# Reordering VectorE's instructions in the first batch of a fused attention and mixture-of-experts kernel

## The chip, the cores and the metric

The kernel runs on one core of one Trainium2 chip. The metric is the device time of one execution in microseconds, the median of several runs. The core's engines work side by side and wait for each other by semaphores: TensorE (matmul), VectorE, ScalarE, GpSimd, and SyncE, which here only starts transfers.

## The reference

The input x has 4 images of 128 channels and 32 × 32 points. Three blocks follow each other, all in float32:

```
h = group_norm(x)                      # 32 groups, eps 1e-6, scale and bias per channel
q, k, v = nin(h, Wq, bq), nin(h, Wk, bk), nin(h, Wv, bv)
w = softmax(q^T k * C**-0.5)           # 1024 x 1024 per image
x = x + nin(w v, Wp, bp)
t = tokens(x)                          # (4, 1024, 128)
t = t + linear_attention(layer_norm(t))      # 4 heads of 32, softmax of the keys over the tokens
t = t + top2_of_8_experts(layer_norm(t))     # gelu(t w1 + b1) w2 + b2, weighted by the router
```

## The kernel before

The work is ordered by hand. Each engine has its own program, written out in the order in which the engine is to work, and each of them has an `opening_batch` for image 0, a `batch` for images 1 to 3, and a last part with the experts. Semaphores link the engines; an engine that reaches a wait stops there with all that stands behind it.

Products of full precision are made of three matmuls with operands split in a high and a low part. ScalarE makes the high part out of PSUM (q_hi, k_hi, v_hi, pT_hi), then VectorE subtracts it to get the low part (q_lo, k_lo in `project`, L1037; v_lo in `project_v`, L1028; pT_lo in `turn_probs`, L1059). k_hi and k_lo are the two halves of one tile, k_both, so rows name them k_both. Halves of 512 points are named by a digit: q0, q1, k0, k1.

Attention of one image has 8 row tiles of 128 rows. For row tile i TensorE makes the scores (`score`, six matmuls, L1449 to L1451), VectorE takes scale and row maximum (`row_maximum`, L1052, 128 × 1024), ScalarE the exponential (`softmax`, L720), TensorE transposes the probabilities (T{i}, L1464), ScalarE and VectorE split them (L726, L1059). After tiles 0 to 3's transposes the attention products begin (`attend`). The first score needs the low parts of q0 and k0, its second half that of k1. The score of tile 2 needs the maximum of tile 0.

The group statistics of images 1 to 3 are taken in image 0 on VectorE: `group_stats(b)` is two BN_STATS (L935) on x of image b, held in the tiles gel, hs and out_s. They go into one `channel_means(1, 3)` (L941) after the third, then over TensorE (group_means) and back to VectorE (group_deviation, group_variance, group_affine), and from there to GpSimd, which normalizes image 1. `setup_rest` (L1019 to L1022) takes the router's rows and b1 out of the PSUM bank in which TensorE turned them (rowsT); the second half of the transposed x (xT1) goes into the same bank and waits for that. TensorE's order there is: scores 0 and 1, v, T0, score 2, rowsT, T1, x transposed (xT0, xT1), score 3, T2, score 4, the group means, T3, the group variances, score 5, attend.

Of the kernel before, what the change touches and what calls it, by code (L numbers as in the profile page):

```python
# [132 lines left out]
def conv_attention_moe(nc, x, gn_scale, gn_bias, wq, bq, wk, bk, wv, bv, wp, bp,  # L133
# [28 lines left out]
    with ctx:  # L162
# [170 lines left out]
        def ps(place, unit):  # L333
            bank = place.bank(unit)
            return ring[:, bank, :] if bank < 4 else scores[:, bank - 2, :]

        def wait_filled(eng, place, unit):
            eng.wait_ge(filled[place.bank(unit)], place.earlier(unit) + 1)
# [13 lines left out]
        def half(m, n):  # L352
            return m[:, n * BANK:(n + 1) * BANK]
# [559 lines left out]
        def _(dve):  # L913
# [3 lines left out]
            def after(ins):  # L917
                made[0] += 1
                ins.then_inc(dve_chain, 1)
                dve.wait_ge(dve_chain, made[0])  # L920
# [11 lines left out]
            def group_stats(b):  # L932
                for n in range(HALVES):
                    dve.wait_ge(ld_x0b if (b, n) == (0, 1) else ld_x[b], 16)
                    last = dve.bn_stats(gst[:, b, n, :], half(x_of[b], n))  # L935
                after(last)

            def channel_means(b0, nb):

                for b in range(b0, b0 + nb):  # L940
                    last = dve.bn_aggr(gmv[:, b, :], gst[:, b, :, :])  # L941
                last.then_inc(gn_mv, 1)

            def group_deviation(place, b0, nb):

                mean, dev = gsum[:, 0, b0:b0 + nb], gsum[:, 1, b0:b0 + nb]
                wait_filled(dve, place, "gn_mean")
                dve.tensor_copy(mean, ps(place, "gn_mean")[:, 0:nb]).then_inc(drained[place.bank("gn_mean")], 1)
                wait_drained(dve, place, "gn_mean")
                after(dve.tensor_tensor(dev, gmv[:, b0:b0 + nb, 0], mean, ALU.subtract))  # L950
                after(dve.tensor_tensor(dev, dev, dev, ALU.mult))
                dve.tensor_tensor(dev, dev, gmv[:, b0:b0 + nb, 1], ALU.add).then_inc(gn_mv, 1)

            def group_variance(place, b0, nb):
                wait_filled(dve, place, "gn_var")
                dve.tensor_copy(gsum[:, 2, b0:b0 + nb], ps(place, "gn_var")[:, 0:nb]
                                ).then_inc(drained[place.bank("gn_var")], 1)

            def group_affine(n, b0, nb):

                dve.wait_ge(gn_rstd, n)
                after(dve.tensor_scalar(gmul[:, b0:b0 + nb], gsum[:, 3, b0:b0 + nb], gs_c, None, ALU.mult))
                after(dve.tensor_tensor(gadd[:, b0:b0 + nb], gsum[:, 0, b0:b0 + nb], gmul[:, b0:b0 + nb], ALU.mult))
                dve.tensor_scalar(gadd[:, b0:b0 + nb], gadd[:, b0:b0 + nb], -1.0, gb_c, ALU.mult, ALU.add
                                  ).then_inc(gn_made, 1)
# [35 lines left out]
            def weights_again():  # L1001

                split(wq_raw, wq_hi[:, :], wq_lo[:, :])
                split(wk_raw, wk_hi[:, :], wk_lo[:, :])
# [11 lines left out]
            def setup_rest():  # L1016

                wait_filled(dve, FIRST, "rowsT")
                dve.tensor_copy(b1_c[:, :], ps(FIRST, "rowsT")[:, E:2 * E])  # L1019
                dve.tensor_copy(router_top[:, 0:E], ps(FIRST, "rowsT")[:, 0:E])  # L1020
                after(dve.tensor_copy(router_two[:, 0:E], ps(FIRST, "rowsT")[:, 0:E]))
                dve.tensor_tensor(router_two[:, E:2 * E], ps(FIRST, "rowsT")[:, 0:E],  # L1022
                                  router_two[:, 0:E].bitcast(FP32), ALU.subtract).then_inc(drained[FIRST.bank("rowsT")], 1)

            def low(place, unit, hi, lo, made, count):

                dve.wait_ge(made, count)
                dve.tensor_tensor(lo, ps(place, unit)[:, 0:lo.shape[-1]], hi.bitcast(FP32), ALU.subtract  # L1028
                                  ).then_inc(drained[place.bank(unit)], 1)

            def project(place, b, unit, hi, lo, bias):
                n = int(unit[1])
                if place is FIRST:
                    bias = bias_first[:, 0:1] if unit[0] == "q" else bias_first[:, 1:2]

                dve.wait_ge(qk_hi_made, b * 4 + ATTENTION["qk"].index(unit) + 1)
                dve.scalar_tensor_tensor(out=half(lo, n), in0=ps(place, unit), scalar=bias,  # L1037
                                         in1=half(hi, n).bitcast(FP32), op0=ALU.add, op1=ALU.subtract
                                         ).then_inc(drained[place.bank(unit)], 1)

            def project_v(place, b):
                for n in range(HALVES):
                    low(place, f"v{n}", half(v_hi, n), half(v_lo, n), v_hi_made, b * HALVES + n + 1)

            def row_maximum(place, b, i):

                if i >= 2:
                    wait_filled(dve, place, f"T{i - 2}b")
                elif place is not FIRST:
                    wait_filled(dve, place, f"T{TILES - 2 + i}b")  # L1050
                dve.wait_ge(s_made, b * TILES + i + 1)
                dve.tensor_scalar(prob[:, i % 2, :],  # L1052
                                  scores[:, 2 * (i % 2):2 * (i % 2) + 2, :].rearrange("p a t -> p (a t)"),
                                  -SCALE, None, ALU.mult, ALU.min, accum_out=row_max[:, i:i + 1]).then_inc(s_max, 1)

            def turn_probs(place, b, i):
                for n, unit in enumerate((f"T{i}a", f"T{i}b")):
                    dve.wait_ge(p_hi_made, b * (2 * TILES) + 2 * i + n + 1)
                    dve.tensor_tensor(tile_group(pT_lo, n, i), as_tiles(ps(place, unit)),  # L1059
                                      tile_group(pT_hi, n, i).bitcast(FP32), ALU.subtract  # L1060
                                      ).then_inc(drained[place.bank(unit)], 1)

            def invert_sums(b, g):

                dve.wait_ge(s_exp, b * TILES + (g + 1) * QUAD)
                dve.reciprocal(row_sum[:, 1, g * QUAD:(g + 1) * QUAD], row_sum[:, 0, g * QUAD:(g + 1) * QUAD]
                               ).then_inc(r_made, 1)
# [150 lines left out]

            def opening_batch(place, b):
                project(place, b, "q0", q_hi, q_lo, bq_c)  # L1220
                group_stats(1)
                project(place, b, "k0", k_hi, k_lo, bk_c)
                project(place, b, "k1", k_hi, k_lo, bk_c)
                group_stats(2)
                project(place, b, "q1", q_hi, q_lo, bq_c)
                row_maximum(place, b, 0)
                row_maximum(place, b, 1)
                project_v(place, b)
                turn_probs(place, b, 0)
                row_maximum(place, b, 2)  # L1230
                setup_rest()
                turn_probs(place, b, 1)
                group_stats(3)
                channel_means(1, B - 1)
                row_maximum(place, b, 3)
                turn_probs(place, b, 2)
                group_deviation(place, 1, B - 1)
                turn_probs(place, b, 3)
                group_variance(place, 1, B - 1)
                row_maximum(place, b, 4)  # L1240
                invert_sums(b, 0)
                group_affine(2, 1, B - 1)
                weights_again()
                row_maximum(place, b, 5)
                turn_probs(place, b, 4)
                row_maximum(place, b, 6)
                turn_probs(place, b, 5)
                row_maximum(place, b, 7)
                dve.wait_ge(experts_split, 3)
                residual(place, b, 0)  # L1250

            def batch(place, b, la, lc):
# [57 lines left out]
                take_g(place)  # L1310

            opening_batch(FIRST, 0)
            batch(SECOND, 1, 0, None)
            with dve.Fori(2, B) as b:
# [572 lines left out]
```

## Time and profile before

| | |
|---|---|
| median of 3 runs | 318.69 us (318.09 to 318.78) |
| span of the profiled execution, first to last instruction | 315.6 us |
| TensorE matmul busy | 297.7 us, 94% |
| VectorE busy | 254.9 us, 81% |
| ScalarE busy | 200.8 us, 64% |
| GpSimd busy | 154.1 us, 49% |
| granted TensorE clock, mean | 1.000 |

A profile describes one execution; for this one the page gives its span and no device time of its own. Times in rows count from the span's start. "Busy" is time in which an instruction was in work. Instructions of one engine overlap a little at their ends, so the time an instruction takes of its engine is the distance from its start to the next start, when nothing waits.

### The profile page before, as it was taken

The numbers are of one execution on the slowest core, as the hardware profiler recorded it, in microseconds if no ns is written. First come the engines' busy times: TensorE is split into PE (matmuls) and PEld (weight loads), VectorE is DVE, ScalarE is ACT, GpSimd is POOL, SyncE is SP. The second block draws the span as 40 slices with busy tenths as digits, with TensorE's granted clock in tenths as the row PEclk, the third lists the DMA queues.
The fourth block names the chain that finished last, engine by engine and source line by source line (L and its number), as shares of the span: only waits on it lengthen the run. The fifth ranks groups of instructions, "written<-read, shape, count | busy, mean of one in ns | idle before, by whom it ended". The sixth has DMA issues, their size and how long they took to land.

```text
span 315.6 us, 5504 instructions
## 1 busy us (share of the span) xinstructions
PE 297.7 (94%) x1584; PEld 238.3 (76%) x1584; DVE 254.9 (81%) x635; ACT 200.8 (64%) x352; POOL 154.1 (49%) x358
## 2 busy tenths in 40 slices
PE   5898989989999999999999999998799998999996
PEld 4776768866878887878887797875677786668885
DVE  4599686587587799987698887999598896999996
ACT  3447474566771587663279577468578645888882
POOL 2899593059941985980784300599604049200000
PEclk9999999999999999999999999999999999999999
DMA  5902000010000021000000118395321783229801
GB/s 136 330 12 70 0 1 2 0 66 2 1 3 0 0 69 39 30 12 0 0 1 0 66 38 271 117 391 212 124 86 67 279 300 119 75 87 375 295 7 66
DMA packets 12904, 29.61 MB, mean 94 GB/s; under 512 B 2208, under 2 KB 6224, under 8 KB 10960
## 3 DMA queue, kind: packets, MB, share of 16 engines
q1 hardware_dynamic: 12448, 28.87, 26.3%
q10 hardware_dynamic: 432, 0.46, 0.4%
q8 instruction: 10, 0.16, 0.2%
q14 instruction: 14, 0.11, 0.1%
HBM read 24.73 MB, written 4.59 MB: 93 GB/s over the span
## 4 chain that ended last, share of the span: by engine, by line
PE 66%; DVE 13%; POOL 9%; ACT 7%; issue 3%; DMA 1%; DVEq 0%; POOLq 0%
PE ring L1464 11%; PE ring L1449 7%; PE ring L1451 7%; PE ring L1450 7%; PE scores L1449 6%; PE scores L1451 6%; PE scores L1450 6%; POOL w_n L589 3%; PE ring L1805 3%; POOL u L589 3%; ACT pT_hi L726 3%; ACT prob L720 2%; PE ring L1604 2%; DVE pT_lo L1059 2%; PE ring L1591 2%
## 5 line engine op out<-in xcount | busy, mean ns | idle before, releaser
L867 ACT ACTIVATE gel<-scores,b_c 128x512 f32<-128x512 f32 x64 | 43.9, 689 | 19.5 <-PE scores L1451 18.0
L1059 DVE TENSOR_TENSOR pT_lo<-ring,pT_hi 128x512 fp32r<-128x512 f32 x64 | 40.5, 681 | 9.8 <-ACT pT_hi L726 9.4
L720 ACT ACTIVATE prob<-prob,row_max 128x1024 f32<-128x1024 f32 x32 | 36.8, 1149 | 14.2 <-DVE prob L1052 14.2
L580 POOL TENSOR_SCALAR rstd<-lmv 128x4 f32<-128x4 f32 x16 | 4.3, 266 | 82.3 <-DVE lmv L1094 81.1
L1052 DVE TENSOR_SCALAR_CACHE_REDUCE prob<-scores 128x1024 f32<-128x1024 f32 x32 | 38.6, 1214 | 3.3 <-PE scores L1451 3.3
L726 ACT ACTIVATE pT_hi<-ring 128x512 fp32r<-128x512 f32 x64 | 34.6, 599 | 10.3 <-PE ring L1464 9.9
L1464 PE MATMUL ring<-ident,prob 128*128 128x128 f32 x256 | 33.7, 275 | 3.6 <-ACT prob L720 1.9
L1464 PEld LDWEIGHTS ring<-ident,prob 128*128 128x128 f32 x256 | 28.7, 140 | 8.5 <-ACT prob L720 3.7
L1449 PE MATMUL scores<-wT_hi,w_hi 128*128 128x512 f32 x64 | 29.3, 458 | 0.0
L1449 PE MATMUL scores<-k_both,q_hi 128*128 128x512 f32 x64 | 26.9, 421 | 1.9 <-DVE k_both L1037 1.3
L1449 PE MATMUL ring<-pT_hi,v_hi 128*128 128x512 f32 x64 | 26.5, 415 | 0.8 <-DVE pT_lo L1059 0.8
L1451 PE MATMUL scores<-k_both,q_lo 128*128 128x512 f32 x64 | 25.2, 393 | 0.0
L1451 PE MATMUL scores<-wT_hi,w_lo 128*128 128x512 f32 x64 | 25.1, 392 | 0.0
L1450 PE MATMUL scores<-wT_lo,w_hi 128*128 128x512 f32 x64 | 25.1, 392 | 0.0
L1450 PE MATMUL scores<-k_both,q_hi 128*128 128x512 f32 x64 | 25.1, 392 | 0.0
L1451 PE MATMUL ring<-pT_hi,v_lo 128*128 128x512 f32 x64 | 25.0, 391 | 0.0
L1450 PE MATMUL ring<-pT_lo,v_hi 128*128 128x512 f32 x64 | 25.0, 390 | 0.0
L611 POOL TENSOR_TENSOR t<-t,bout_row 128x128 f32<-128x128 f32 x32 | 14.0, 476 | 18.4 <-PE scores L1464 10.8
L730 ACT ACTIVATE o_s<-ring 128x512 f32<-128x512 f32 x8 | 4.8, 598 | 24.7 <-PE ring L1451 24.7
L589 POOL TENSOR_SCALAR u<-t,rstd 128x128 f32<-128x128 f32 x32 | 18.8, 608 | 0.9 <-POOL rstd L584 0.9
L589 POOL TENSOR_SCALAR w_n<-t,rstd 128x128 f32<-128x128 f32 x32 | 17.2, 555 | 0.9 <-POOL rstd L584 0.9
L584 POOL TENSOR_TENSOR rstd<-rstd,minus_half 128x4 f32<-128x4 f32 x16 | 16.6, 1040 | 0.0
(300 smaller groups left out, 780.9 us busy)
## 6 DMA issues: line engine op xcount, KB each, us to landing
pT_hi<-scratch_s SPq DMA_DIRECT2D x8, 1024.0 KB, 7.6
prob<-scratch_s SPq DMA_DIRECT2D x4, 1024.0 KB, 7.2
k_both<-scratch_s SPq DMA_DIRECT2D x3, 1024.0 KB, 5.8
z_in<-scratch_z SPq DMA_DIRECT2D x8, 256.0 KB, 2.9
out_dram<-out_s SPq DMA_DIRECT2D x7, 256.0 KB, 2.2
xb<-in_x_dram SPq DMA_DIRECT2D x3, 512.0 KB, 3.3
scratch_z<-out_s SPq DMA_DIRECT2D x2, 512.0 KB, 2.8
k_both<-scratch_s SPq DMA_DIRECT2D x4, 256.0 KB, 4.2
```

The lines of the kernel that those rows point to most:

```text
L584: pool.tensor_tensor(std[:, tiles], std[:, tiles], minus_half[:, tiles], ALU.pow).then_inc(ln_small[n], 1)
L589: last = pool.tensor_scalar(dst[:, j, :], src[:, j, :], neg[:, j:j + 1], std[:, j:j + 1], ALU.add, ALU.mult)
L611: last = pool.tensor_tensor(tiles_piece(t2, n), tiles_piece(t1, n), tiles_piece(bout_b, n), ALU.add)
L720: act.activation(prob[:, i % 2, :], prob[:, i % 2, :], ACT.Exp, bias=row_max[:, i:i + 1], scale=-1.0, accum_out=row_sum[:, 0, i:i + 1]).th ...
L726: act.activation(tile_group(pT_hi, n, i), as_tiles(ps(place, unit)), ACT.Copy).then_inc(p_hi_made, 1)
L867: act.activation(half(gel, s % 2), scores[:, s % 2, :], ACT.Gelu, bias=b1_c[:, s % E:s % E + 1]).then_inc(e_gelu, 1)
L1052: dve.tensor_scalar(prob[:, i % 2, :], scores[:, 2 * (i % 2):2 * (i % 2) + 2, :].rearrange("p a t -> p (a t)"), -SCALE, None, ALU.mult, AL ...
L1059: dve.tensor_tensor(tile_group(pT_lo, n, i), as_tiles(ps(place, unit)), tile_group(pT_hi, n, i).bitcast(FP32), ALU.subtract).then_inc(drai ...
L1449: pe.matmul(dst, lh, rh, start=start, stop=False)
L1450: pe.matmul(dst, lh, rl, start=False, stop=False)
L1451: return pe.matmul(dst, ll, rh, start=False, stop=stop)
L1464: last = pe.transpose(dst[0:t.shape[-1], j * step:j * step + rows], t, ident[0:rows, 0:rows])
```

## The change

VectorE's program for image 0 is written in another order. The low parts of k0 and k1 come directly after that of q0, the maximum of row tile 0 ahead of q1's low part, and the statistics of images 1 and 2 after the maximum of tile 1 and after that of tile 2. All other engines keep their order, and no instruction's work changes.

```diff
             def opening_batch(place, b):
                 project(place, b, "q0", q_hi, q_lo, bq_c)
-                group_stats(1)
                 project(place, b, "k0", k_hi, k_lo, bk_c)
                 project(place, b, "k1", k_hi, k_lo, bk_c)
-                group_stats(2)
+                row_maximum(place, b, 0)
                 project(place, b, "q1", q_hi, q_lo, bq_c)
-                row_maximum(place, b, 0)
                 row_maximum(place, b, 1)
+                group_stats(1)
                 project_v(place, b)
                 turn_probs(place, b, 0)
                 row_maximum(place, b, 2)
+                group_stats(2)
                 setup_rest()
                 turn_probs(place, b, 1)
                 group_stats(3)
```

VectorE's order before, from q0's low part to the maximum of row tile 3 (gel and hs hold x of images 1 and 2):

```order
L1037 SCALAR_TENSOR_TENSOR q_lo<-ring,bias_first,q_hi 128x512
L935 BN_STATS gst<-gel 128x6 x2
L1037 SCALAR_TENSOR_TENSOR k_both<-ring,bias_first,k_both 128x512 x2
L935 BN_STATS gst<-hs 128x6 x2
L1037 SCALAR_TENSOR_TENSOR q_lo<-ring,bias_first,q_hi 128x512
L1052 TENSOR_SCALAR prob,row_max<-scores 128x1024 x2
L1028 TENSOR_TENSOR v_lo<-ring,v_hi 128x512 x2
L1059 TENSOR_TENSOR pT_lo<-ring,pT_hi 128x4x128 x2
L1052 TENSOR_SCALAR prob,row_max<-scores 128x1024
L1019 COPY b_c<-ring 128x8
```

The same place after the change, up to the same row:

```order
L1037 SCALAR_TENSOR_TENSOR q_lo<-ring,bias_first,q_hi 128x512
L1037 SCALAR_TENSOR_TENSOR k_both<-ring,bias_first,k_both 128x512 x2
L1052 TENSOR_SCALAR prob,row_max<-scores 128x1024
L1037 SCALAR_TENSOR_TENSOR q_lo<-ring,bias_first,q_hi 128x512
L1052 TENSOR_SCALAR prob,row_max<-scores 128x1024
L935 BN_STATS gst<-gel 128x6 x2
L1028 TENSOR_TENSOR v_lo<-ring,v_hi 128x512 x2
L1059 TENSOR_TENSOR pT_lo<-ring,pT_hi 128x4x128 x2
L1052 TENSOR_SCALAR prob,row_max<-scores 128x1024
L935 BN_STATS gst<-hs 128x6 x2
L1019 COPY b_c<-ring 128x8
```

Both pairs of statistics moved down past TensorE's first scores, and both still stand ahead of the router's rows (the COPY) and so ahead of the maximum of row tile 3, which follows further down in both. In between, these rows stand in both:

```order
L1022 TENSOR_TENSOR router_two<-ring,router_two 128x8
L1059 TENSOR_TENSOR pT_lo<-ring,pT_hi 128x4x128 x2
L935 BN_STATS gst<-out_s 128x6 x2
L941 BN_AGGR gmv<-gst 128x2 x3
L1052 TENSOR_SCALAR prob,row_max<-scores 128x1024
```

Nothing moved there.

## Rows read from the trace of the kernel before

**Rows 1.** The page: the span, and what each engine was busy.

```profile
span 315.6 us, 5504 instructions
PE 297.7 (94%) x1584; PEld 238.3 (76%) x1584; DVE 254.9 (81%) x635; ACT 200.8 (64%) x352; POOL 154.1 (49%) x358
```

**Rows 2.** The chain of waits from 12 to 32 us: start, us, what.

```profile
13.95 0.29 DVE gst L935
...
28.80 1.09 ACT pT_hi L726 x2
29.88 1.13 ACT prob L720 x2
```

**Rows 3.** VectorE in order of time, image 0: start, us, instruction, idle before it.

```profile
13.20 0.75 DVE L1037 SCALAR_TENSOR_TENSOR q_lo<-ring,bias_first,q_hi 128x512 fp32r<-128x512 f32 x1 [0.97 <-ACT q_hi L709]
13.86 1.28 DVE L935 BATCH_NORM_STATS2 gst<-gel 128x6 f32<-128x512 f32 x2
15.18 1.41 DVE L1037 SCALAR_TENSOR_TENSOR k_both<-ring,bias_first,k_both 128x512 fp32r<-128x512 f32 x2
16.50 1.28 DVE L935 BATCH_NORM_STATS2 gst<-hs 128x6 f32<-128x512 f32 x2
...
18.48 1.21 DVE L1052 TENSOR_SCALAR_CACHE_REDUCE prob<-scores 128x1024 f32<-128x1024 f32 x1
...
20.77 0.08 DVE L1052 DVE_READ_ACCUMULATOR prob<-scores 128x1 f32 x1
21.49 1.29 DVE L1028 TENSOR_TENSOR v_lo<-ring,v_hi 128x512 fp32r<-128x512 f32 x2 [0.65 <-ACT v_hi L715]
...
23.89 1.22 DVE L1052 TENSOR_SCALAR_CACHE_REDUCE prob<-scores 128x1024 f32<-128x1024 f32 x1
...
25.04 0.16 DVE L1019 COPY b_c<-ring 128x8 f32<-128x8 f32 x1
...
28.23 1.17 DVE L1052 TENSOR_SCALAR_CACHE_REDUCE prob<-scores 128x1024 f32<-128x1024 f32 x1
...
32.39 1.29 DVE L1059 TENSOR_TENSOR pT_lo<-ring,pT_hi 128x512 fp32r<-128x512 f32 x2 [0.89 <-ACT pT_hi L726]
```

**Rows 4.** ScalarE in order of time: k's high parts, exponentials of tiles 0, 3.

```profile
13.49 1.39 ACT L709 ACTIVATE k_both<-ring,bias_first 128x512 fp32r<-128x512 f32 x2 [0.33 <-PE ring L1451]
...
19.74 1.15 ACT L720 ACTIVATE prob<-prob,row_max 128x1024 f32<-128x1024 f32 x1 [4.17 <-DVE prob L1052]
...
29.77 1.15 ACT L720 ACTIVATE prob<-prob,row_max 128x1024 f32<-128x1024 f32 x1
```

**Rows 5.** TensorE's matmuls in order of time: projection, then score of tile 0.

```profile
12.49 0.63 PE L1450 MATMUL ring<-h_lo,wk_hi 128*128 128x512 f32 x1
...
12.92 0.47 PE L1451 MATMUL ring<-h_hi,wk_lo 128*128 128x512 f32 x1
...
16.07 0.47 PE L1449 MATMUL scores<-k_both,q_hi 128*128 128x512 f32 x1 [1.29 <-DVE k_both L1037]
...
17.31 0.40 PE L1451 MATMUL scores<-k_both,q_lo 128*128 128x512 f32 x1
```

**Rows 6.** Later, a score's last matmul and the maximum that waited for it.

```profile
86.45 0.39 PE L1451 MATMUL scores<-k_both,q_lo 128*128 128x512 f32 x1
86.98 1.23 DVE L1052 TENSOR_SCALAR_CACHE_REDUCE prob<-scores 128x1024 f32<-128x1024 f32 x1 [0.66 <-PE scores L1451]
```

**Rows 7.** TensorE's weight loads: xT1, score 3, T2, first attention product.

```profile
25.60 0.42 PEld L1464 LDWEIGHTS ring<-ident,xb 128*128 128x128 f32 x4 [0.20 <-DVE router_two L1022]
25.98 0.19 PEld L1449 LDWEIGHTS scores<-k_both,q_hi 128*128 128x128 f32 x1
...
28.10 0.85 PEld L1464 LDWEIGHTS ring<-ident,prob 128*128 128x128 f32 x8 [0.88 <-issue]
...
33.73 0.19 PEld L1449 LDWEIGHTS ring<-pT_hi,v_hi 128*128 128x128 f32 x1 [0.39 <-DVE pT_lo L1059]
```

**Rows 8.** GpSimd in order of time: it takes up image 1's columns.

```profile
35.91 0.29 POOL L540 COPY affine<-gmul 128x1 f32<-128x1 f32 x1 [0.93 <-DVE gadd L964]
```

## The prediction

> **What bounds the kernel now.** The page comes first: TensorE is at work for 94% of a span of 315.6 us [rows 1]. Yet a share over the whole span says nothing about the first 30 us, which is all that the change touches, so I went to the chain of waits for that stretch. It is an unbroken run of pieces: statistics on VectorE at 13.95, the keys' low parts, the first maxima, and by the end ScalarE's conversion of row tile 2 at 28.80 and its exponential of row tile 3 behind it, ending at 31.01 [rows 2]. The chain's last two pieces on ScalarE hide something that the third view, VectorE alone in order of time, shows. VectorE stands still once between 13.20 and 28.23: for 0.65 us, waiting for the high part of v [rows 3]. Counted from the start of one instruction to the start of the next, that wait is 21.49 − 20.77 = 0.72 us. No other row of VectorE in that stretch has idle time ahead of it. TensorE, in contrast, idles 1.29 us ahead of its first score [rows 5]. So VectorE sets the pace here, and the key quantity is how long VectorE stands still, not how early any one thing is made.
>
> How near is ScalarE behind it? The maximum of tile 3 starts at 28.23. In a place where ScalarE waits for nothing else, the exponential starts 19.74 − 18.48 = 1.26 us after its maximum [rows 3, 4], so the exponential of tile 3 could have begun at 29.49. It begins at 29.77, behind the conversion of tile 2. ScalarE covers 0.28 us of VectorE lateness, no more (0.33 if I count this maximum's own, shorter duration of 1.17 us against 1.21).
>
> **The change, part by part.** Nothing is added or removed. VectorE's instructions are the same, so its work from 13.20 to the maximum of tile 3 is the same 15.03 − 0.72 = 14.31 us. Both moved pairs of statistics (1.32 us a pair, 15.18 − 13.86 [rows 3]) still stand ahead of that maximum, because group_stats(3), channel_means and the maximum of tile 3 keep their places. Its new start therefore depends only on the new waits:
>
> 1. The low part of k0 follows the low part of q0 directly. VectorE is free at 13.86, but ScalarE makes k0's high part from 13.49 and k1's behind it, 1.39 us for both, so the first is there at 14.18 and the second at 14.88 [rows 4]. With 0.03 us for the hand-over, my estimate, k0 starts at 14.21 (wait 0.35 us) and k1 at 14.91, where 14.21 + 0.66 = 14.87 would be possible (wait 0.04 us; 0.66 is half of 16.50 − 15.18). Before, they ran from 15.18.
> 2. The first score waits for k0: before, the low part started at 15.18 and the score at 16.07, 0.89 us later [rows 3, 5]. Now 14.21 + 0.89 = 15.10. Its last matmul starts 17.31 − 16.07 = 1.24 us later, at 16.34. From a score's last matmul to its maximum there are 86.98 − 86.45 = 0.53 us in the one place of these rows where VectorE really waited for it [rows 6]. The maximum of tile 0 starts at about 16.86. VectorE was free at 14.91 + 0.66 = 15.57: wait 1.29 us. This is the stretch that the statistics used to fill.
> 3. Then q1's low part and the maximum of tile 1 follow at once, since score 1 starts its last matmul at 15.10 + 1.5 + 1.24 = 17.84 and allows its maximum at 18.37, while VectorE comes to it at 16.86 + 1.21 + 0.66 = 18.7. The first exponential starts at 16.86 + 1.26 = 18.12 instead of 19.74. The statistics of batch 1 then take VectorE to 21.2 (another 1.21 and 1.32), by when v's high part is long done (before, VectorE could take it 21.49 − 19.74 = 1.75 us after that exponential began, so now from 19.87): the old 0.72 us wait is gone.
> 4. Sum of waits after: 0.35 + 0.04 + 1.29 = 1.68 us, against 0.72. VectorE is 0.96 us behind the old order from there on. The maximum of tile 2 still gains, as one statistics pair now stands behind it: 23.89 + 0.96 − 1.32 = 23.53. Everything after that pair loses: the router's rows 25.04 → 26.00, the maximum of tile 3 28.23 → 29.19.
> 5. The exponential of tile 3 starts at 29.19 + 1.26 = 30.45, or 30.40 with the shorter duration, instead of 29.77: **0.63 to 0.68 us later**.
>
> TensorE's own path has to be checked too, since it waits for the router's rows before it turns the second half of x: weight load at 25.60, score 3 at 25.98, tile 2's transposes at 28.10 [rows 7]. Now 26.56, 26.94 and, with 1.5 us for a score, 28.44. The conversion of tile 2 then starts at about 29.14 and clears ScalarE at 30.1, 0.3 us ahead of the exponential. It doesn't set the time, but it is only 0.3 us away.
>
> From 30.4 on the old schedule repeats, shifted. The exponential releases tile 3's transposes, these the conversion, this VectorE's low part at 32.39 (VectorE idle 0.89 us there, so its 0.96 us of lateness is not added on top), and this the attention products, for which TensorE waits 0.39 us at 33.73 [rows 3, 7]. The same VectorE stretch then gives the affine columns for which GpSimd waits 0.93 us before it normalizes batch 1 [rows 8]. Both ways into the rest of the program shift alike, and the chain from there to the end is connected, with no clock-time event such as an early load to wait for. So I carry the 0.65 us undiminished: 315.6 + 0.65 = 316.25 us of span. The runs' median lies 3.09 us above the span; **318.69 + 0.65 = 319.34 us**. The page's row has no other time of its execution, so the span and this difference are the base.
>
> **The rivals.**
>
> *The head start is kept (not slower).* Place: VectorE's wait ahead of the maximum of tile 0. ScalarE's cover of 0.28 us makes a sum of waits of up to 0.72 + 0.28 = 1.00 us free; for that the wait on score 0 would have to be 0.6 us instead of 1.29. Then the time stays at 318.7 us. For it speaks that this wait is built from two hand-overs seen once each, and that the exponentials of tiles 0 and 1 do come over a microsecond earlier. Against it stand the 1.24 us of score 0 itself, which nothing shortens. A real gain needs something more, namely that the tile 3 exponential follows its forerunners; if the 1.0 us by which they lead survived, the time would be 317.7 us, but that asks VectorE to be done with the same work 1.0 us earlier than before, while it waits longer.
>
> *Part of the shift is absorbed.* The chain has pieces marked "issue" for which the profile shows no cause, and such pieces could shrink. Then 0 to 0.4 us remain: 318.7 to 319.1 us.
>
> *TensorE slows down.* In the new order TensorE, after tile 1's transposes and the first half of x, waits for the router's rows until 26.56. Before, that wait began at 25.60 − 0.20 = 25.40 [rows 7]; TensorE now comes to it 0.4 to 1.6 us sooner (the leads of the maximum of tile 2 and of the exponential of tile 0), say 1.2, so it idles 2.4 us instead of 0.20. Early in the trace, matmuls of this size start 12.92 − 12.49 = 0.43 us apart, the pitch of the 1.2 GHz level, against 1.24 / 5 = 0.25 in the first score [rows 5], the pitch of the 2.4 GHz level plus a late start. At the slow pitch, score 3 (six matmuls) costs 1.2 us more and the eight transposes some 0.4; less the 0.3 us of room, the shift grows by about 1.3 us: 320.6 us. Against it: idle of 1.29 us left the first score fast. The Trainium skill's page "TensorE: Matmul & The Clock Gate", Part 1 (The HAM clock gate), says that the array's rate is set by how busy it has been lately, and warns of idle gaps; by this rule the time could be the 320.6 us of this case. No row shown here has a gap of 2.4 us, so the trace of before neither bears the rule out nor speaks against it at this size.
>
> **How the numbers follow.** A difference of 0.2%, 0.64 us, is about what a measurement of this kernel can tell, and my sum ends just on it. The shift of 0.65 us undiminished has 0.74, of which slightly more than half reads as slower (0.39) and the rest as no change (0.35). Head start kept: 0.10, half of it a gain over 0.2%, half none. Absorbed in part: 0.09, no change. TensorE slows or something else makes it worse: 0.07, slower. That gives faster 0.05, same 0.49, slower 0.46. The range: unknowns of step 2 (the 0.53 us, by where VectorE catches the score) and of ScalarE's cover are ±0.15 us, the three runs of before spread over 0.7 us. To leave out no more than 2 in 10 it reaches to 318.5 below (absorbed, with the spread) and 320.0 above.
>
> **What would show it.** Right: k's low parts start near 14.2 and 14.9, the first score near 15.1, the maximum of tile 0 near 16.9 with a wait of about 1.3 us on the score ahead of it; no wait at v; TensorE idle over 2 us before the second half of x; the exponential of tile 3 near 30.4, now released by its maximum. Wrong: a maximum of tile 3 ahead of 28.9, or an unequal shift at 33.73 and at the end. A span under 315.6 would mean that the chain wasn't bound to VectorE where I say.

## The result, and the profile after

The changed kernel takes 320.88 us (median of 10 executions, 319.10 to 322.01) against 318.43 us for the kernel before beside it (10 executions, 317.08 to 319.89). The ratio is 1.0058, 95% interval 1.0033 to 1.0083: slower by 0.6%, where 0.2% was forecast. The two medians alone are 2.45 us apart (0.8%); the text goes by the ratio and its interval. The profiled execution has a span of 319.2 us against 315.6 us.

The first lines of the page, busy tenths in 40 slices of 8 us:

```profile
span 319.2 us, 5504 instructions
...
PE   5997998989999999999999999997899998999996
...
PEclk9997999999999999999999999999799999999999
```

TensorE's granted clock is no longer full everywhere: it falls in the fourth slice (24 to 32 us) and in the 29th (223 to 231 us). The row of before has 9 in all 40 slices. Over 24 to 32 us the mean granted clock is 0.79 here and 1.00 before. So the reader goes to TensorE in the fourth slice. Its matmuls in order of time, start, duration, idle ahead:

```profile
15.13 0.47 PE L1449 MATMUL scores<-k_both,q_hi 128*128 128x512 f32 x1 [0.34 <-DVE k_both L1037]
...
26.50 0.77 PE L1464 MATMUL ring<-ident,xb 128*128 128x128 f32 x4 [2.17 <-DVE router_two L1022]
26.91 0.78 PE L1449 MATMUL scores<-k_both,q_hi 128*128 128x512 f32 x1
27.49 0.63 PE L1450 MATMUL scores<-k_both,q_hi 128*128 128x512 f32 x1
27.92 0.63 PE L1451 MATMUL scores<-k_both,q_lo 128*128 128x512 f32 x1
...
29.62 1.38 PE L1464 MATMUL ring<-ident,prob 128*128 128x128 f32 x8
30.76 0.48 PE L1449 MATMUL scores<-k_both,q_hi 128*128 128x512 f32 x1
31.07 0.39 PE L1450 MATMUL scores<-k_both,q_hi 128*128 128x512 f32 x1
```

The first score starts 0.94 us earlier [rows 5], as meant. Then TensorE waits 2.17 us for the router's rows, and score 3 behind that wait runs with 0.43 us between starts (27.92 − 27.49), the pace of the 1.2 GHz level, until about 30.3; the mean granted clock from 26.5 to 30.3 us is 0.55. VectorE in order of time:

```profile
14.23 1.44 DVE L1037 SCALAR_TENSOR_TENSOR k_both<-ring,bias_first,k_both 128x512 fp32r<-128x512 f32 x2 [0.39 <-ACT k_both L709]
16.80 1.23 DVE L1052 TENSOR_SCALAR_CACHE_REDUCE prob<-scores 128x1024 f32<-128x1024 f32 x1 [1.13 <-PE scores L1451]
...
21.07 1.29 DVE L1028 TENSOR_TENSOR v_lo<-ring,v_hi 128x512 fp32r<-128x512 f32 x2
...
25.93 0.17 DVE L1019 COPY b_c<-ring 128x8 f32<-128x8 f32 x1
...
28.86 0.35 DVE L941 BATCH_NORM_AGGREGATE gmv<-gst 128x2 f32<-128x12 f32 x3
29.95 1.23 DVE L1052 TENSOR_SCALAR_CACHE_REDUCE prob<-scores 128x1024 f32<-128x1024 f32 x1 [0.74 <-PE scores L1451]
```

Up to the router's rows each start is within 0.1 us of the forecast (14.21, 16.86, no wait at v, 26.00). The maximum of tile 3 could have started at about 29.1 (forecast 29.19), but the slow score holds it until 29.95. On ScalarE:

```profile
18.07 1.15 ACT L720 ACTIVATE prob<-prob,row_max 128x1024 f32<-128x1024 f32 x1 [2.50 <-DVE prob L1052]
...
30.60 1.09 ACT L726 ACTIVATE pT_hi<-ring 128x512 fp32r<-128x512 f32 x2 [2.70 <-PE ring L1464]
31.57 1.15 ACT L720 ACTIVATE prob<-prob,row_max 128x1024 f32<-128x1024 f32 x1
```

Tile 0's exponential gains 1.67 us, tile 3's loses 31.57 − 29.77 = 1.80 us [rows 4]. From there the shift is carried rigidly for the next 57 us. The attention product on TensorE's weight loads, GpSimd's columns, and a maximum much later on VectorE:

```profile
35.53 0.19 PEld L1449 LDWEIGHTS ring<-pT_hi,v_hi 128*128 128x128 f32 x1 [0.39 <-DVE pT_lo L1059]
```

```profile
37.71 0.29 POOL L540 COPY affine<-gmul 128x1 f32<-128x1 f32 x1 [0.93 <-DVE gadd L964]
```

```profile
88.78 1.22 DVE L1052 TENSOR_SCALAR_CACHE_REDUCE prob<-scores 128x1024 f32<-128x1024 f32 x1 [0.66 <-PE scores L1451]
```

All three stand exactly 1.80 us later than in [rows 6, 7, 8], with the same idle time ahead of them. The span is 3.6 us longer, so the other 1.8 us have another origin: 0.2 us come in by 222 us (222.69 before, 224.68 after), without a cause found, and 1.6 us right behind that. Near 220 us TensorE waits 2.1 us for GpSimd, in both kernels. First before, then after:

```profile
222.69 0.66 PE L1464 MATMUL ring<-ident,u 128*128 128x128 f32 x4 [2.09 <-POOL u L589]
...
223.42 0.40 PE L1450 MATMUL scores<-wT_lo,w_hi 128*128 128x512 f32 x1
```

```profile
224.68 0.97 PE L1464 MATMUL ring<-ident,u 128*128 128x128 f32 x4 [2.08 <-POOL u L589]
...
225.88 0.63 PE L1450 MATMUL scores<-wT_lo,w_hi 128*128 128x512 f32 x1
```

The same wait, yet the slow pace follows only in the second. The change has no instruction near this wait. Is the fall chance of the execution? Only the mean granted clock is on record for every execution. The profiled executions with one such stretch have a mean of 0.994 or 0.995, the one with two has 0.989, so the others are counted by their means: 0.993 to 0.995 as one stretch, 0.988 or 0.989 as two. The mean doesn't say where the stretch lies.

| kernel | executions | clock 0.998 or more | one stretch | two |
|---|---|---|---|---|
| before (all comparisons below) | 84 | 26 | 53 | 5 |
| changed | 10 | 1 | 4 | 5 |

In the comparisons below, before has spans of 315.2 to 317.0 us at full clock and a median of 317.1 to 317.3 us over all. The profile of before that the prediction used was thus one of the fastest executions, not the typical one; its time would lie 1.7 to 2.2 us above its span, as in all profiled executions of the experiments, not 3.09.

### The profile page after: what moved, and what is told of

It reads as the page before. It is cut to its first block, busy times and chain, and to the rows that moved or that the text cites. A ratio compares the mean times of both kernels' runs of the same rounds, so it can differ in the third digit from the quotient of the medians.

```text
span 319.2 us, 5504 instructions
## 1 busy us (share of the span) xinstructions
PE 300.8 (94%) x1584; PEld 240.8 (75%) x1584; DVE 254.4 (80%) x635; ACT 200.6 (63%) x352; POOL 153.8 (48%) x358
## 4 chain that ended last, share of the span: by engine, by line
PE 65%; DVE 14%; POOL 9%; ACT 4%; issue 3%; DMA 3%; SPq 1%; DVEq 0%; POOLq 0%; ACTq 0%
PE ring L1464 11%; PE ring L1449 7%; PE ring L1451 7%; PE ring L1450 7%; PE scores L1449 7%; PE scores L1451 6%; PE scores L1450 6%; POOL w_n L589 3%; PE ring L1805 3%; POOL u L589 3%; DVE prob L1052 2%; ACT pT_hi L726 2%; DVE pT_lo L1059 2%; PE ring L1604 2%; PE ring L1591 2%
## 5 line engine op out<-in xcount | busy, mean ns | idle before, releaser
L1464 PEld LDWEIGHTS ring<-ident,prob 128*128 128x128 f32 x256 | 29.2, 142 | 7.5 <-ACT prob L720 3.3
L1449 PE MATMUL scores<-k_both,q_hi 128*128 128x512 f32 x64 | 27.5, 429 | 1.0 <-DVE prob L1052 0.7
L1450 PE MATMUL scores<-k_both,q_hi 128*128 128x512 f32 x64 | 25.6, 400 | 0.0
```

Of the source, the lines that this page charges most:

```text
L1449: pe.matmul(dst, lh, rh, start=start, stop=False)
L1450: pe.matmul(dst, lh, rl, start=False, stop=False)
L1464: last = pe.transpose(dst[0:t.shape[-1], j * step:j * step + rows], t, ident[0:rows, 0:rows])
```

## The experiments

The theory after the result: TensorE's longer idle ahead of xT1 costs it the clock in most executions (1.1 us), and VectorE's longer waits cost the rest (0.65 us). The rivals: the fall has another cause in the new order and would stay if the idle were filled; or the new order's place for the keys is what costs. A ratio below is always to before on the same chip, with its 95% interval.

**e1: TensorE kept busy in the early idle.**

```diff
-                turn_x(place, b)
+                pe.wait_ge(xb_made, b + 1)
+                turn(place, "xT0", [tile(xb, j) for j in range(QUAD)])
+                pe.wait_ge(s_max, 2)
+                for _ in range(16):
+                    pe.matmul(scores[:, 2, 0:C], group_mean[:, :], ident[:, :], start=True, stop=True)
+                turn(place, "xT1", [tile(xb, QUAD + j) for j in range(QUAD)])
```

> The changed kernel, with 16 small matmuls added on TensorE between the two halves of x's transposes, where it stood idle for 2.17 us; their output is overwritten. Theory (the idle costs the clock): all matmuls of score 3 start 0.23 us apart, granted clock 1.00 from 24 to 32 us, the maximum of tile 3 starts near 29.2 with no wait on the score, the exponential of tile 3 near 30.4 (changed kernel 31.57, before 29.77), and the time falls by about 1.1 us against the changed kernel, to 0.65 us above before. Rival (the slow stretch has another cause than this idle): the clock is still 0.79 there and the exponential stays near 31.5.

Measured: ratio 1.0064 (1.0042 to 1.0086), span of the profile 317.8 us. The filling missed its size: the 16 products became 32 matmuls. TensorE in the profile:

```profile
24.74 3.74 PE L1687 MATMUL scores<-ident,group_mean 128*128 128x128 f32 x32
28.32 0.60 PE L1464 MATMUL ring<-ident,xb 128*128 128x128 f32 x4
28.67 0.48 PE L1449 MATMUL scores<-k_both,q_hi 128*128 128x512 f32 x1
28.99 0.39 PE L1450 MATMUL scores<-k_both,q_hi 128*128 128x512 f32 x1
```

3.74 us of filling in place of 1.9 delayed xT1 to 28.32, so the time says nothing. The pace does: score 3 ran at full speed although it came 1.8 us later than in the changed kernel. It is repeated with half the filling as e7.

**e2: the router's rows ahead of image 2's statistics.**

```diff
                 row_maximum(place, b, 2)
+                setup_rest()
                 group_stats(2)
-                setup_rest()
```

> The changed kernel with the statistics of image 2 behind the router's rows instead of ahead of them, so that VectorE's work up to the maximum of tile 3 and its waits stay the same and only TensorE's wait for the rows shrinks from 2.17 to about 0.85 us. Theory: no fall of the clock; the exponential of tile 3 starts near 30.4, held by the maximum of tile 3 (29.2), so 0.65 us above before. Rival: the loss of the changed kernel comes from VectorE's order as such, so that the time stays near the changed kernel's, 1.8 us above before.

Measured: ratio 1.0024 (0.9998 to 1.0050); six of 12 executions at full clock with spans of 316.3 to 317.8 us. TensorE's wait and the third maximum on VectorE:

```profile
25.57 0.66 PE L1464 MATMUL ring<-ident,xb 128*128 128x128 f32 x4 [0.85 <-DVE router_two L1022]
...
26.30 0.40 PE L1450 MATMUL scores<-k_both,q_hi 128*128 128x512 f32 x1
```

```profile
29.53 1.17 DVE L1052 TENSOR_SCALAR_CACHE_REDUCE prob<-scores 128x1024 f32<-128x1024 f32 x1
```

With 0.85 us of idle the clock holds, and by the ratios the loss is less than half of the change's, though the two intervals overlap. The maximum stands 0.3 us later than expected (29.2); why, the section below says.

**e3: only image 2's statistics moved**, from ahead of q1 to behind the maximum of tile 2.

```diff
                 project(place, b, "k1", k_hi, k_lo, bk_c)
-                group_stats(2)
                 project(place, b, "q1", q_hi, q_lo, bq_c)
...
                 row_maximum(place, b, 2)
+                group_stats(2)
                 setup_rest()
```

> Before, with only the statistics of image 2 moved behind the maximum of tile 2. Theory: VectorE waits 0.7 us for score 0 and 0.7 us for v, 1.4 us in all against 0.72; the maximum of tile 3 starts near 28.9 and the exponential near 30.15, 0.4 us above before, if the clock holds. TensorE's wait for the router's rows is near 1.5 us; whether the clock falls after it is open. If it falls, the exponential starts near 31.2. Rival (waits of VectorE don't matter): the exponential at 29.8.

Measured: ratio 1.0026 (0.9997 to 1.0054); the exponential of tile 3 at 30.19 in the profile (expected 30.15), behind its maximum at 28.98. TensorE idled 1.18 us ahead of xT1 there and kept its pace.

**e4: only image 1's statistics moved**, behind the maximum of tile 1.

```diff
                 project(place, b, "q0", q_hi, q_lo, bq_c)
-                group_stats(1)
                 project(place, b, "k0", k_hi, k_lo, bk_c)
...
                 row_maximum(place, b, 1)
+                group_stats(1)
```

> Before, with only the statistics of image 1 moved behind the maximum of tile 1, so that the keys' low parts come first and the statistics of image 2 still fill the wait for score 0. Theory: VectorE waits 0.39 us in all instead of 0.72, the maximum of tile 3 starts near 27.9, the exponential near 29.15, held by its maximum or by the conversion of tile 2: 0.5 to 0.6 us faster than before, clock 1.00. Rival (the head start of the keys is what costs): 0.3 us or more slower than before.

Measured: ratio 1.0016 (0.9998 to 1.0035), so neither the gain of 0.5 us nor the full clock came. The profile has the exponential of tile 3 at 29.30, 0.47 us ahead of before, but 0.18 us of that is an execution that began earlier (q0's low part at 13.02 against 13.20), and VectorE's idle time was 0.58 us, not the expected 0.39, against 0.65 before; its maximum of tile 3 at 28.09 gained nothing by the order. The clean case is e8 below. All 12 executions show one stretch at the lower clock, in the profile the late one near 222 us. That led to filling the late idle.

**e5 and e6: the late idle filled**, in before (e5) and in the changed kernel (e6), by 8 products into the bank that TensorE is about to use.

```diff
+            def padded_u(la, n):
+                if n == 1:
+                    dst = open_unit(TAIL, "u1")
+                    for _ in range(8):
+                        pe.matmul(dst[:, 0:C], group_mean[:, :], ident[:, :], start=True, stop=True)
+                turn_u(TAIL, la, n)
...
-                *((TAIL_AT["u" + str(n)], lambda n=n: turn_u(TAIL, la, n)) for n in range(2)),
+                *((TAIL_AT["u" + str(n)], lambda n=n: padded_u(la, n)) for n in range(2)),
```

> Before, with 8 small products (16 matmuls, about 1.85 us) added on TensorE while it waits 2.09 us near 220.6 us for GpSimd's normalized tile u; their output is overwritten. Theory (idle of about 2 us on TensorE costs it the clock in some executions and not in others): 22 of 32 executions of before show a mean clock of 0.995 or less, here all show 1.000, and the span's median falls from about 317.1 to about 315.9 us. Rival (the clock falls for another cause): the same mixture of clocks as before.

> The changed kernel with the same 16 matmuls in the late idle. Theory: one fall of the clock is left, the early one behind the 2.17 us wait for the router's rows, in 9 of 10 executions (0.995); span 317.4 us where it falls, 1.8 above the matching kernel before without any fall (315.6 to 315.9). Rival: 0.989 stays as frequent as before this edit (5 of 10).

**e7: both idles filled in the changed kernel**: the edit of e1 with `range(8)`, and that of e6.

> The changed kernel with both idles filled, the early one now with 8 products (16 matmuls, 1.87 us), which end before the router's rows are taken. Theory: clock 1.000 in all executions, the exponential of tile 3 near 30.4 (not 31.57), the maximum of tile 3 without a wait, span 316.3 to 316.5 us, so 0.65 us above before with its late idle filled; this is what VectorE's longer waits cost by themselves. Rival: the early fall of the clock stays, or the difference to before is gone.

**e8: e4 with the late idle filled.**

> Only the statistics of image 1 moved (as in the kernel that does this alone), with the late idle filled. In that kernel's profile the exponential of tile 3 started at 29.30, 0.47 us ahead of before, and all 12 executions showed the late fall of the clock. Theory: clock 1.000, span 315.2 to 315.5 us, the fastest of all, about 1.5 us below the median of before. Rival: the clock still falls and the median stays near 317.1 us.

These four were compared together, 8 to 12 executions each:

| kernel | ratio to before | interval | median us | one slow stretch |
|---|---|---|---|---|
| e5, before + late idle filled | 0.9969 | 0.9948 to 0.9991 | 317.95 | 1 of 12 |
| e6, changed + late idle filled | 1.0015 | 0.9986 to 1.0043 | 319.55 | 8 of 12 |
| e7, changed + both filled | 0.9977 | 0.9956 to 0.9997 | 318.63 | 0 of 12 |
| e8, only image 1's statistics + late filled | 0.9949 | 0.9924 to 0.9973 | 317.52 | 0 of 8 |

Before itself had 22 of 31 executions with one or two slow stretches in these comparisons. Filling the late idle takes them away in all but one. In the changed kernel 8 of 12 remain, and filling the early idle takes away these. The theory holds in both places. The spans' medians came out 0.3 to 0.4 us above what was expected of e5, e7 and e8 (316.25, 316.9 and 315.75 us).

The profile of e6 is one of the 4 executions that kept the clock behind the same idle:

```profile
27.16 0.65 PE L1464 MATMUL ring<-ident,xb 128*128 128x128 f32 x4 [2.16 <-DVE router_two L1022]
27.57 0.48 PE L1449 MATMUL scores<-k_both,q_hi 128*128 128x512 f32 x1
```

Its score 3 takes 1.48 us up to T2 (27.57 to 29.05), that of the changed kernel 2.71 us (26.91 to 29.62).

With image 1's statistics alone moved (e8), VectorE idles 0.33 us in place of before's 0.65, and its maximum of tile 3 is 0.3 us earlier; the exponential follows at 29.14 against 29.77:

```profile
27.93 1.17 DVE L1052 TENSOR_SCALAR_CACHE_REDUCE prob<-scores 128x1024 f32<-128x1024 f32 x1
```

In e7, TensorE and VectorE read:

```profile
24.99 1.95 PE L1687 MATMUL scores<-ident,group_mean 128*128 128x128 f32 x16
27.32 0.44 PE L1464 MATMUL ring<-ident,xb 128*128 128x128 f32 x2 [0.38 <-DVE router_two L1022]
```

```profile
14.53 0.75 DVE L1037 SCALAR_TENSOR_TENSOR k_both<-ring,bias_first,k_both 128x512 fp32r<-128x512 f32 x1 [0.42 <-ACT k_both L709]
15.81 0.75 DVE L1037 SCALAR_TENSOR_TENSOR k_both<-ring,bias_first,k_both 128x512 fp32r<-128x512 f32 x1 [0.53 <-ACT k_both L709]
17.62 1.22 DVE L1052 TENSOR_SCALAR_CACHE_REDUCE prob<-scores 128x1024 f32<-128x1024 f32 x1 [1.07 <-PE scores L1451]
...
29.95 1.17 DVE L1052 TENSOR_SCALAR_CACHE_REDUCE prob<-scores 128x1024 f32<-128x1024 f32 x1
```

The filling delays nothing and the clock is full, but the maximum of tile 3 is at 29.95 and the exponential at 31.17, not 30.4. VectorE idles three times ahead of the first maximum, 2.02 us in all, where the changed kernel's profile has 1.52 (0.39 + 1.13). The new item is the 0.53 us for k1's high part. TensorE shows where it comes from, in e7 and in e5:

```profile
13.51 0.63 PE L1449 MATMUL ring<-h_hi,wk_hi 128*128 128x512 f32 x1
13.93 0.63 PE L1450 MATMUL ring<-h_lo,wk_hi 128*128 128x512 f32 x1
```

```profile
13.23 0.63 PE L1449 MATMUL ring<-h_hi,wk_hi 128*128 128x512 f32 x1
13.66 0.63 PE L1450 MATMUL ring<-h_lo,wk_hi 128*128 128x512 f32 x1
```

In both executions k1's projection still runs at the lower level, where in the profiles of before and of the changed kernel it already ran at 0.23 us a matmul: TensorE's first rise to full clock came at 15.1 us in e7 and 14.6 in e5, against 13.1 and 13.3 in those two. This first rise is read from the matmuls' pace alone: the row of the granted clock shows 9 in the first slices of every profile, so a mean of 1.000 says nothing about it. In e5, with the order of before, nothing comes of it; VectorE:

```profile
18.36 1.21 DVE L1052 TENSOR_SCALAR_CACHE_REDUCE prob<-scores 128x1024 f32<-128x1024 f32 x1
...
21.38 1.29 DVE L1028 TENSOR_TENSOR v_lo<-ring,v_hi 128x512 fp32r<-128x512 f32 x2 [0.65 <-ACT v_hi L715]
```

These are the starts of [rows 3], 0.1 us earlier. The statistics ahead of the keys gave TensorE and ScalarE time for a late k1; the new order has no such slack, so that an execution with a late rise pays 0.4 to 0.7 us more. Executions also begin up to 0.4 us apart (q0's low part at 13.02 to 13.40), so the distance is counted from q0's low part. In the five profiles with the changed kernel's order up to there, the maximum of tile 0 starts 3.71 us behind it (changed kernel, rise at 13.3), 4.13 (e2, 14.3), 4.26 (e1, 15.2), 4.27 (e7, 15.1) and 4.37 (e6, 16.0). In e1, e2 and e7 the second half of score 0 waits for k1's low part; in e6 TensorE itself is late, for score 0 starts straight behind q1's projection at the slow pace. That is also the 0.3 us missed in e2.

**e9: VectorE's wait for score 0 filled by image 1's statistics**, the router's rows ahead of image 2's as in e2, and the late idle filled as in e6.

```diff
                 project(place, b, "k1", k_hi, k_lo, bk_c)
+                group_stats(1)
                 row_maximum(place, b, 0)
                 project(place, b, "q1", q_hi, q_lo, bq_c)
                 row_maximum(place, b, 1)
-                group_stats(1)
                 project_v(place, b)
                 turn_probs(place, b, 0)
                 row_maximum(place, b, 2)
+                setup_rest()
                 group_stats(2)
-                setup_rest()
```

> The changed kernel with the statistics of image 1 put back ahead of the maximum of tile 0, where VectorE waits over 1 us for score 0, those of image 2 behind the router's rows, and TensorE's late idle filled. Theory (the loss is VectorE's wait for score 0, and any ready work of 1.3 us fills it): VectorE waits under 0.8 us in all, the maximum of tile 3 starts at 28.0 to 28.3, the exponential at 29.3 to 29.5, 1.6 us or more ahead of the changed kernel with both idles filled (31.17 in its profile), clock 1.000, median near 317.6 us. Rival (the place of the keys' low parts costs, whatever stands behind them): the exponential after 30.4 and the median near 318.6.

Measured: ratio 0.9972 (0.9952 to 0.9991), median 318.02 us, like e5 (0.9969). The maximum of tile 3 is at 28.61 in the profile and the exponential at 29.82, 0.3 us later than expected, in an execution that began as late as e7's (q0's low part at 13.40), and 1.35 us ahead of e7. VectorE idles 0.65 us, as in before. The median missed the expected 317.6 by 0.4 us. The keys may come first at no cost that these runs resolve, if work stands behind them; the rival falls.

**e10: before, with the router's rows late.** No part of the change is in it, except that TensorE is made to wait; the late idle is filled.

```diff
                 row_maximum(place, b, 2)
-                setup_rest()
                 turn_probs(place, b, 1)
                 group_stats(3)
+                setup_rest()
                 channel_means(1, B - 1)
```

> Before, with the router's rows taken later on VectorE, behind tile 1's low parts and the statistics of image 3, and with TensorE's late idle filled. Nothing of the change is in it; it only makes TensorE wait, from about 25.4 to 28.1, for 2.7 us. The same kernel without this showed a mean clock of 0.995 in 1 of 12 executions. Theory (an idle of TensorE of more than 2 us here loses it the clock): most executions show 0.995, score 3's matmuls start 0.43 us apart, the exponential of tile 3 starts near 33 us. Rival (the clock falls by something else in the new order): clock 1.000 in nearly all, the exponential near 31.8.

Measured: ratio 1.0073 (1.0042 to 1.0105); 9 of 11 executions show the slow stretch, against 1 of 12 in e5. TensorE in the profile:

```profile
28.22 0.99 PE L1464 MATMUL ring<-ident,xb 128*128 128x128 f32 x4 [2.88 <-DVE router_two L1022]
...
29.44 0.63 PE L1450 MATMUL scores<-k_both,q_hi 128*128 128x512 f32 x1
29.86 0.63 PE L1451 MATMUL scores<-k_both,q_lo 128*128 128x512 f32 x1
```

An idle in this place, without the new order, brings the fall of the clock. The same execution also has a shorter idle that kept it, ahead of its first score, whose third matmul starts 0.23 us behind the second (16.09):

```profile
15.79 0.47 PE L1449 MATMUL scores<-k_both,q_hi 128*128 128x512 f32 x1 [1.80 <-DVE k_both L1037]
...
16.32 0.39 PE L1451 MATMUL scores<-k_both,q_lo 128*128 128x512 f32 x1
```

The exponential of tile 3 was at 33.30 (expected near 33).

## Why the prediction was wrong

1. **VectorE's new waits, 1.68 us against 0.72.** Right in the profiled execution to 0.1 us at each step. The key quantity was right too: how long VectorE stands still, not how early a tile is made. Over profiles with different orders, the maximum of tile 3 starts 14.4 to 14.8 us after q0's low part, plus VectorE's idle time between them:

| profile | idle, us | from q0's low part to the maximum of tile 3 | less the idle |
|---|---|---|---|
| e8 | 0.33 | 14.76 | 14.43 |
| before | 0.65 | 15.03 | 14.38 |
| e9 | 0.65 | 15.21 | 14.56 |
| e3 | 1.06 | 15.82 | 14.76 |
| changed, had score 3 been in time (29.13) | 1.52 | 16.04 | 14.52 |
| e7 | 2.02 | 16.60 | 14.58 |

2. **"The shift of 0.65 us undiminished", carried from tile 3 to the end.** The carrying was right: 1.80 us at 31.57, 35.53, 37.71 and 88.78, and 1.99 at 224.68. The size at tile 3 was not: 1.80 us in place of 0.65.
3. **TensorE's path in the main sum ("Now 26.56, 26.94 and, with 1.5 us for a score, 28.44"). This is the step that failed.** The sum lets score 3 run at full pace behind a longer wait and so puts a fall of the clock at nothing; the fall stood only in the rival "TensorE slows down", which with anything else that makes it worse was given 0.07. The runs show that score 3 took 2.71 us behind 2.17 us of idle, against 1.48 us in e6's profile, that this held the maximum of tile 3 from 29.13 to 29.95, and that it happens in 8 of 12 executions. The rival's place (the wait for the router's rows), idle (2.4 us, measured 2.17), mechanism and price (0.65 + 1.3, measured 1.80) were right. That its 320.6 us comes near the measured 320.88 is in part luck: over before beside it the rival has 1.95 us and the medians 2.45, with late stretches in both kernels of which the prediction knew nothing. "Idle of 1.29 us left the first score fast" was no evidence for 2.2 us. The trace of before also held a wait of 2.09 us from 220.6 us, which the prediction left out and which kept the clock in that one execution; over 84 executions about 7 in 10 lose it there or elsewhere. The rule cited from the Trainium skill's "TensorE: Matmul & The Clock Gate", Part 1, is borne out in its direction by e5, e6, e7 and e10; the idle gaps that it warns of are longer than those of 2.17 and 2.88 us that cost the clock here. In the profiles, idles of 0.85 us (e2), 1.18 us (e3) and 1.80 us (e10, first score) kept the clock, 2.17 and 2.88 us lost it, and 2.16 us kept it in the profile of e6.
4. **k1's high part at a fixed time (step 1 of the sum).** Mis-sized: it was read off one execution with an early rise of the clock. With a late rise the forecast 16.86 becomes 17.2 to 17.6.
5. **"315.6 us and 3.09 us more".** Wrong base: 315.6 us was an execution at full clock, 1.5 to 1.7 us under the median of before. It didn't change the difference, but it hid that both kernels have slow stretches.

What the 0.6% is made of: e6 against e5, the change with the late idle filled in both, is 1.6 us by the medians, 1.5 by the ratios. The early slow stretch (e6 against e7) has 0.9 us of the medians; 8 of 12 against 0 of 12 is clear, but its price in the medians is not (−0.2 to 1.3 us, a 95% interval from resampling the executions). VectorE's waits (e7 against e5) have 0.7 us (0.1 to 1.4 us in the same way), but only 0.25 us by the two ratios (1.0008), so their size stays open. The rest up to the 0.58% of the ratio, some 0.4 us, is not assigned. It may lie in the late stretch, and whether an earlier shift alters the odds of that one is open as well: 12 of 12 executions of e4 show one stretch, 3 of 9 of e1, against 58 of 84 of before.

e8 beats both kernels, 0.9949 (0.9924 to 0.9973). Most of that is the filled late idle (e5); what the moved statistics add over e5, 0.4 us by the medians, is not clear of noise.

## What to carry to other kernels

On an engine that paces a stretch, count how long it stands still in the new order; work moved away from a wait has to be replaced by other ready work. Then look where TensorE will idle longer. Here idles up to 1.8 us kept the clock in the profiles, those of 2.1 us or more lost it in most executions, and nothing in between was measured. Give the fall of the clock the chance that many executions show, not that of one trace. A few products without use into a free bank cost nothing there, as long as they end before the wait does (0.22 us ahead in e5; in e1, twice as many held xT1 back to 28.32). And take the trace of one execution as one draw: what was read at a late or early rise of the clock can be 0.5 us off in the next.

## What else the runs showed

The same wait of TensorE near 220 us, 2.0 to 2.1 us in the six profiles in which it isn't filled, was followed by the lower clock in two of them (changed, e4) and not in four (before, e1, e2, e3), with the same work ahead of it. What decides it in one execution, these runs don't show. Also not forecast is a spread of under 1 us at full clock: in the profile of e7 VectorE waits at 196 us for a load of the experts' shares, in the profile of before the same wait is 0.81 us, at 193.7.

```profile
196.39 0.69 DVE L1335 TENSOR_TENSOR hs<-gel,k_both 128x512 f32<-128x512 f32 x1 [2.07 <-DMA k_both<-scratch_s]
```

TensorE's shift against the profile of before grows from 1.40 us (at 193.07 there) to 2.24 (at 203.13) in that execution, which accounts for most of the 0.9 us by which e7's profiled span (317.8 us) is above its median (316.9).
